# A Mamba-2 mixer with its state stepped every 64 tokens in place of every 128

## What is computed

```
proj = x @ in_proj_w.T            # gate, x|B|C, dt
hBC  = silu(causal_conv4(proj[x|B|C]))
dt   = clip(softplus(dt + dt_bias));  A_cum = cumsum(dt * A) in a chunk
Y_diag = (C_l . B_s) * exp(A_cum[l]-A_cum[s]) * (s<=l) @ (x*dt)
states = sum_s B_s * exp(A_cum[-1]-A_cum[s]) * (x*dt)_s
prev'  = prev * exp(A_cum[-1]) + states
Y_off  = exp(A_cum[l]) * (C_l @ prev)
y = (Y_diag + Y_off + D*x) * silu(gate);  y = group_rms_norm(y) @ out_proj_w.T
```

## Time and profile before

| | us |
|---|---|
| median of 3 runs | 1868.56 (1868.19 to 1874.12) |
| time of the profiled execution | 1870.32 |
| its span, first to last instruction | 1868.5 |
| mean granted TensorE clock | 0.988 |

### The profile page before, as it was taken

How to read it: one execution, slowest core, us unless ns; L and a number is a source line. 1 busy time by engine, 2 the same in 40 slices (tenths; PEclk the granted TensorE clock), 3 DMA queues, 4 the chain that set the end, 5 groups by cost and what they waited for, 6 DMA issues and landing times.

```text
span 1868.5 us, 31134 instructions
## 1 busy us (share of the span) xinstructions
PE 1754.7 (94%) x9656; PEld 1344.0 (72%) x9656; DVE 1290.5 (69%) x2095; ACT 1065.5 (57%) x1946; POOL 942.1 (50%) x721
## 2 busy tenths in 40 slices
PE   6799999999999999999999999999999999999966
PEld 5567777777777777777777777777777777777755
DVE  5766667666766677766676667666777666766788
ACT  6566555656646565665546566465656555565632
POOL 2355453556535464554535555355644545455563
PEclk9899999999999999999999999999999999999988
DMA  6412121111202121121211212121211212111121
GB/s 224 130 30 69 55 66 44 50 60 57 66 28 72 49 66 51 35 66 55 66 45 48 62 54 68 29 72 45 70 51 29 72 55 66 44 48 61 34 96 57
DMA packets 77097, 114.14 MB, mean 61 GB/s; under 512 B 21376, under 2 KB 28032, under 8 KB 76032
## 3 DMA queue, kind: packets, MB, share of 16 engines
q1 hardware_dynamic: 59360, 80.06, 14.2%
q10 hardware_dynamic: 17568, 31.99, 5.1%
HBM read 88.94 MB, written 23.07 MB: 60 GB/s over the span
## 4 chain that ended last, share of the span: by engine, by line
issue 46%; POOL 34%; PE 9%; DVE 5%; ACT 3%; DMA 1%; SPq 1%; POOLq 1%; ACTq 0%; DVEq 0%
POOL yt L1605 9%; POOL ssq L1600 7%; POOL wg_lo L1524 4%; POOL wo_lo L1524 4%; POOL prev L1586 3%; POOL yt L1608 3%; POOL wx_lo L1524 3%; PE bank L476 2%; PE bank L478 2%; PE bank L477 2%; PE bank L641 1%; PE bank L706 1%; DMA raw_w<-w_in_dram 1%; PE bank L840 1%; ACT lm L1072 0%
## 5 line engine op out<-in xcount | busy, mean ns | idle before, releaser
L1605 POOL TENSOR_TENSOR yt<-yt,ea 128x384 f32<-128x384 f32 (+1 forms) x128 | 189.6, 1481 | 393.1 <-DVE ea L1440 393.1
L1218 DVE SCALAR_TENSOR_TENSOR xc<-bank,bpar,xc 128x511 f32<-128x511 f32 (+2 forms) x384 | 285.4, 743 | 52.8 <-ACT xc L906 48.3
L1410 DVE TENSOR_TENSOR lm<-lm,cbm 128x512 f32<-128x512 f32 x256 | 185.9, 767 | 155.7 <-ACT lm L1075 155.7
L476 PE MATMUL bank<-h_hi,wg_hi 128*128 128x512 f32 x640 | 262.0, 409 | 31.3 <-ACT gate L1030 21.9
L478 PE MATMUL bank<-h_hi,wg_lo 128*128 128x512 f32 x640 | 251.0, 392 | 0.0
L477 PE MATMUL bank<-h_lo,wg_hi 128*128 128x512 f32 x640 | 250.2, 391 | 0.0
L476 PE MATMUL bank<-wo_hi,g_hi 128*128 128x512 f32 x496 | 206.9, 417 | 7.2 <-POOL wo_lo L1524 7.2
L476 PE MATMUL bank<-h_hi,wx_hi 128*128 128x512 f32 x512 | 210.3, 411 | 2.2 <-DVE bt L1218 2.2
L1586 POOL TENSOR_TENSOR prev<-prev,dec 128x512 f32<-128x512 f32 x96 | 102.0, 1063 | 206.0 <-DVE prev L1356 131.9
L478 PE MATMUL bank<-h_hi,wx_lo 128*128 128x512 f32 x512 | 200.3, 391 | 0.0
L477 PE MATMUL bank<-h_lo,wx_hi 128*128 128x512 f32 x512 | 199.9, 390 | 0.0
(11 more groups left out here) (187 smaller groups left out, 3796.9 us busy)
## 6 DMA issues: line engine op xcount, KB each, us to landing
raw_w<-w_in_dram SPq DMA_DIRECT2D x145, 256.0 KB, 2.6
raw_w<-w_out_dram SPq DMA_DIRECT2D x64, 256.0 KB, 2.6
part_d<-part ACTq DMA_DIRECT2D x64, 256.0 KB, 2.0
part<-part_d ACTq DMA_DIRECT2D x58, 256.0 KB, 2.7
rt<-rows_d SPq DMA_DIRECT2D x256, 8.0 KB
acc<-x_dram SPq DMA_DIRECT2D x8, 256.0 KB, 6.6
acc<-w_mod_dram SPq DMA_DIRECT2D x2, 1024.0 KB, 6.0
lh<-neg_d SPq DMA_DIRECT2D x128, 8.0 KB
```

The costliest lines, as they stand in the source:

```text
L476: nc.tensor.matmul(out_ap, whi(k), hhi(k), start=(k == 0), stop=False)
L1218: stt(dst[:, at], ps[:, 0:HALF - 3 + k], w(k), dst[:, at], ALU.mult, ALU.add)\
L1410: tt(lm[:, h % 4, :], lm[:, h % 4, :], cbm[:, toks(hf)], ALU.mult).then_inc(v_m, 1)
L1605: tt(yt[:, j % 2, cols], yt[:, j % 2, cols], ea[:, j % 2, cols], ALU.add).then_inc(p_t3, 1)
```

## The change

The chunk in which the state is stepped becomes 64 tokens (`SUB`); z still counts 128-token pieces, k counts 64-token pieces, s is the first or second half of a z.

- `diff`: one pair of products per j (two heads, 256 columns each, one row group) in place of two products of 512 columns. Both land in bank 2.
- Relu, Exp and `mix` are one per j in place of two, each still 128 x 512: two heads' 64 x 64 masks lie side by side.
- Masked products: for each z four products of 64 rows, 64 stationary and 64 moving columns, one in each quarter of the array, the token halves to two banks.
- Products with old states: for each 64 tokens one product with 128 stationary and 64 moving columns: 7 or 8 per j in place of 3 or 4.
- State products: for each z two products of 64 rows and 512 columns, in the array's row halves, to banks 6 and 7; now also for z = 3 of the second half (its first 64 tokens).
- DVE: `new_state` 8 or 7 per unit in place of 4 or 3; `xw` also for z = 3; yt in two pieces of 256. POOL: 7 decays per unit in place of 3. SP: 17 small loads per unit in place of 13.
- The C.B products are 16 of 64 x 64 in a group in place of 8 of 128 x 128.

The core of the diff:

```diff
+SUB = CHUNK // 2
+NS = HALF // SUB
...
-        prev = sb("prev", [128, NZ + 1, BLOCK])
-        lm = sb("lm", [128, 4, HALF])
+        prev = sb("prev", [128, NS, BLOCK])
+        lm = sb("lm", [128, 2, HALF])
```

SyncE, `unit_params`:

```diff
+                for j in range(NCT):
+
+                    e = 32 * EA_ROWS[j] + SROWS
+                    rsub = rsrc[j, 0:4, toks(hf)].rearrange("r (z s l) -> s r z l", z=NZ, s=2)
+                    for s in range(2):
+                        at = 32 * j + 4 * s
+                        sp.dma_start(rt[p][at:at + 4, 0:NZ * SUB].bitcast(F).rearrange("r (z l) -> r z l", z=NZ),
+                                     rsub[s]).then_inc(d_par[p], 16)
+                    sp.dma_start(rt[p][e:e + 4, :].bitcast(F), rsrc[j, 4:8, toks(hf)]).then_inc(d_par[p], 16)
```

TensorE, `states`, `diff`, the products with the old states and the masked products:

```diff
+                        te.wait_ge(v_prev, ab0 + 2 * z)
+                    for s in range(1 if hf == 1 and z == NZ - 1 else 2):
+                        lst = nc.tensor.matmul(bank[6 + s][:, :], bt[sub_rows(s), toks(hf, z, 1)],
+                                               xw[sub_rows(s), z % 2, :], start=True, stop=True)
+                    lst.then_inc(t_st, 1)
...
+                    for i in range(2):
+                        lst = nc.tensor.matmul(bank[2][:, i * NZ * SUB:(i + 1) * NZ * SUB],
+                                               lh[par_][32 * j:32 * j + SROWS, i * 128:(i + 1) * 128],
+                                               rt[par_][32 * j:32 * j + SROWS, 0:NZ * SUB], start=True, stop=True)
+                    lst.then_inc(t_diff, 1)
...
-                if hf == 0:
-                    states(3)
+                states(3)
...
-                        te.wait_ge(v_prev, sb0 + 3)
...
+                        te.wait_ge(v_prev, ab0 + NS - 1)
...
-                    for z in range(1 - hf, NZ):
-                        lst = nc.tensor.matmul(bank[6][:, chunk(z)], prev[:, slot(hf, z), j * 128:(j + 1) * 128],
-                                               ct[:, toks(hf, z, 1)], start=True, stop=True)
+                    for k in range(1 - hf, NS):
+                        lst = nc.tensor.matmul(bank[6][:, k * SUB:(k + 1) * SUB],
+                                               prev[:, slot(k), j * 128:(j + 1) * 128],
+                                               ct[:, subtoks(hf, k)], start=True, stop=True)
...
                     for z in range(NZ):
-                        for i in range(2):
-                            h = 2 * j + i
-                            lst = nc.tensor.matmul(bank[5][64 * i:64 * i + 64, chunk(z)],
-                                                   xdt[:, z, h * HDIM:(h + 1) * HDIM], lm[:, h % 4, chunk(z)],
-                                                   start=True, stop=True)
+                        for i, s in ((0, 0), (1, 1), (1, 0), (0, 1)):
+                            h, at = 2 * j + i, (i * NZ + z) * SUB
+                            lst = nc.tensor.matmul(yd[64 * i:64 * i + 64, s, z * SUB:(z + 1) * SUB],
+                                                   xdt[sub_rows(s), z, h * HDIM:(h + 1) * HDIM],
+                                                   lm[sub_rows(s), j % 2, at:at + SUB], start=True, stop=True)
```

VectorE, the order in a unit:

```diff
+                    if z == 3:
+                        new_state(3)
...
                     if z >= 1:
-                        new_state(z - 1)
+                        new_state(2 * z - 2)
...
+                    if z == 1:
+                        new_state(1)
...
                 mix(0)
-                mix(1)
+                new_state(5)
+                new_state(6)
                 if not first and not end:
                     accumulate(u, g1, b1, h1, 3)
                 if hf == 0:
-                    new_state(3)
+                    new_state(7)
```

GpSimd, the order in a unit:

```diff
+                if hf == 1:
+                    decay(0)
+                for f in todo[0] + todo[1]:
+                    unit_fill(f, g)
+                decay(1)
+                decay(2)
+                for f in todo[2]:
+                    unit_fill(f, g)
+                for k in range(3, NS - hf):
+                    decay(k)
+                for f in todo[3]:
+                    unit_fill(f, g)
```

More of the change, by code:

```diff
@@ L327, in _ @@
             xt = x.rearrange("(t p) n -> t p n", p=128)
-            mods = [flat(xdt, 0, 4), flat(gate, 0, 4), flat(prev, 0, 4), flat(lm, 0, 4), flat(acc, 0, 4), flat(acc, 4, 8)]
+            mods = [flat(xdt, 0, 4), flat(gate, 0, 4), flat(prev, 0, 4), flat(prev, 4, 8), flat(acc, 0, 4), flat(acc, 4, 8)]
             def load_mod(v):
@@ L501, in mod_row @@
                 te.wait_ge(d_mod[v], 16)
-                t, k0 = ((xdt, 0), (gate, 0), (prev, 0), (lm, 0), (acc, 0), (acc, 4))[v]
+                t, k0 = ((xdt, 0), (gate, 0), (prev, 0), (prev, 4), (acc, 0), (acc, 4))[v]
                 for k in range(NK):
@@ L630, in unit @@
                 par_, end = hf, last and c == 3
-                sb0 = states_before(nb, hf)
+                ab0 = adds_before(nb, hf)
                 def states(z):
[L634 to L638, removed]
-                    else:
-                        te.wait_ge(v_prev, sb0 + z)
-                    nc.tensor.matmul(bank[7][:, :], bt[:, toks(hf, z, 1)], xw[:, z % 2, :],
-                                     start=True, stop=True).then_inc(t_st, 1)
@@ L644, in diff @@
[L644 to L656 removed]
+                    te.wait_ge(v_xw, 4 * u + z + 1)
@@ L679, in group_bc @@
                     for h2 in range(2):
-                        for zz in range(NZ):
-                            lst = nc.tensor.matmul(bank[2 + h2][:, chunk(zz)], bt[:, toks(h2, zz, 1)],
-                                                   ct[:, toks(h2, zz, 1)], start=True, stop=True)
-                        lst.then_inc(t_cb, 1)
+                        for k in range(NS):
+                            at = (h2 * NZ + k // 2) * SUB
+                            lst = nc.tensor.matmul(bank[2][sub_rows(k % 2), at:at + SUB], bt[:, subtoks(h2, k)],
+                                                   ct[:, subtoks(h2, k)], start=True, stop=True)
+                    lst.then_inc(t_cb, 1)
                     if first:
@@ L970, in _ @@
             keep_row(3)
-            se.wait_ge(v_scan, 2)
-            for z in range(NT):
-                lst = act(ea[:, z // 4, chunk(z % 4)], xw[:, z // 4, chunk(z % 4)], ACT.Exp, scale=-1.0,
-                          bias=xw[:, z // 4, (z % 4 + 1) * 128 - 1:(z % 4 + 1) * 128])
-            lst.then_inc(a_fe, 1)
+            se.wait_ge(v_drop, 1)
+            act(flat(ea, 0, 2), flat(ea, 0, 2), ACT.Exp).then_inc(a_fe, 1)
             pro_split(5)
@@ L1434, in unit @@
                     ge(ve, v_lo, 4 * u + j - 1)
-                    stt(yt[:, j % 2, :], xc[:, j, :], par(c // 2, j, SKIP), bank[5][:, :], ALU.mult, ALU.add)\
-                        .then_inc(v_t2, 1)
+                    for s in range(2):
+                        lst = stt(sub_first(yt[:, j % 2, :])[:, s], sub_first(xc[:, j, :])[:, s], par(c // 2, j, SKIP),
+                                  yd[:, s, 0:NZ * SUB].rearrange("p (z l) -> p z l", z=NZ), ALU.mult, ALU.add)
+                    lst.then_inc(v_t2, 1)
                     ve.wait_ge(t_yo, 4 * u + j + 1)
@@ new lines, in unit @@
+                if not first and c in (0, 3):
+                    group_rstd(g - 1 if c == 0 else g, 1 if c == 0 else 0)
+                if hf == 1:
[10 more added lines that the diff above has]
+                    unit_fill(f, g)
```

217 lines of the change are left out of this document (111 added, 106 removed).

## The result

The changed kernel takes 2056.6 us (median of 4 runs, 2051.4 to 2057.5), the kernel before 1870.7 in the same series: a ratio of 1.0987, 95% interval 1.0958 to 1.1015. That is 186 us slower. The forecast was 1986, with a range to 2055: the direction was right, but the increase was 186 us and not 116, and the time lies just above the range.

A forecast was written before the change was run, and what follows sets the result against it. The prediction took TensorE, busy 94% of the span, to bound the kernel. 1870.3 + 106 of TensorE work + 32 of chain waits - 22 of relieved waits gave 1986 us, range 1945 to 2055.

The forecast's parts named there:

- Old-state products: On TensorE: 1024 more instructions at 0.11 us each, the price of taking up 128 stationary columns, +113 us.
- Rival 4: On TensorE: loads of stationary operands hide whole at any length and shape, 1836 us; chance 0.03.
- State products: On TensorE: row halves run side by side, shape changes cost 38 us and 16 more products 14, +52 us.
- Rival 5: State products on TensorE: the row halves run one after the other, +110, 2096 us; chance 0.03.
- Masked products: On TensorE: eight rounds of four quarters at half the pace save 0.44 us a group, -55 us.
- rivals 2 and 3: Masked products: quarters run only two at a time, 2041 us, chance 0.08; instruction issue bounds them, 2155 us, chance 0.04.
- C.B and row products: On TensorE: C.B products in 16 rounds plus an excursion, -4 us; row products of the differences as long as before, 0.
- Other engines: ScalarE -160 us, VectorE near 1300 to 1340, GpSimd near 1080; none becomes the bound, SP's extra loads are covered.
- The chain at the end of the z phase: TensorE waits 0.4 us for new_state(5) and 0.4 for new_state(6); taken as 1.0 per unit, +32 us.
- The chain within the z phase: Between state products: two links of 3.9 us are covered by 4.4 us of TensorE work, with 0.5 to spare.
- Rival 1: State chain decides: two GpSimd weight splits per unit fall into it, 58 us more, 2044 us; chance 0.17.
- What comes back: On TensorE: waits for VectorE's acc go, -11.0, and half of those on the gate, -11, together -22 us.

The follow-up runs named there:

- before_late_wait: The kernel before, with the first old-state products in first-half units waiting for the unit's last new state: 1892.8 us, ratio 1.0111.
- narrow_alone: The kernel before, with each old-state product cut into two of 64 moving columns, nothing else: 1925.5 us, ratio 1.0292.
- cut_projection: The changed kernel, with the j phase's first projection split ahead of the last state product and the first old-state products: 1987.4 us, ratio 1.0621.
- wide_again: The changed kernel, with old-state products of 128 moving columns again, every second 64 tokens' states left out of them: 1961.0 us, ratio 1.0470.

## Why the prediction was right and wrong

- **Old-state products**, forecast +113: the trace has 28.9 - 15.6 = 13.3 a group, +106. Right. By rows it came from a product with one moving column. The Trainium skill, TensorE: Matmul & The Clock Gate, section LDWEIGHTS (loading the stationary operand), makes it a matter of stationary columns, and the trace agrees with 0.12 us an instruction at 64 moving columns. Rival 4, which let these loads hide, is refuted.
- **State products**, forecast +52: 3.4 a group and 1.2 in the steps into them, +37. The run prices the shape alone: 30, forecast 38. The mechanism was right, the size too high: I gave an excursion 0.4, but a pair takes 0.20 more than a whole product and the step into it 0.10 more, 0.3 together. The Trainium skill, TensorEngine Tiling (Array Packing), section Tiling Modes (Key Properties), says that a change of tiling mode drains the engine; the step of 0.32 in place of 0.22 into a pair agrees. Rival 5 is refuted.
- **Masked products**, forecast -55: -6.3 a group, -50; the run says 47. Right; rivals 2 and 3 are refuted.
- **C.B and row products**, -4 and 0: -0.7 a group and 0.0. Right.
- **Other engines**: none became the bound; SP's four loads cost nothing that the waits show. Right, but ScalarE fell by 110 us, not 160: I took the mean durations of a Relu and an Exp, 0.60 and 0.65, which overlap; by their busy time, 138.8 and 149.2 for 256 each, half of them is 144 at most.
- **The chain at the end of the z phase**: forecast 0.4 and 0.4 us. On the trace TensorE waits 0.4 before the last state product (0.69 from start to start, 764.54 to 765.23, where 0.32 is usual) and 0.44 before the old-state products. Right; the sum took 1.0 a unit, 32 us, where these are about 0.8, 26 us.
- **The chain within the z phase** is the first failed step: "A state product waits for two links, 3.9 us ... so 4.4: covered by 0.5 in the z phase." That took GpSimd as free. In c = 3 the new order puts a third split ahead of `decay(1)`. Rival 1 had named the splits, but at 0.9 us for each of two in every unit, and set against it that "decays 1 and 2 stand ahead of the third split", which is a wrong reading: in c = 3 there are six splits, and the two lists ahead of `decay(1)` hold three. It was one wait of 4.4 us in seven groups, over the 2 us that the prediction named as a sign of being wrong, because the split stands on weights that are late in both kernels. Moving that one loop body was worth 46 us.
- **The clock** is the second and larger failed step. The text says once that the loop ran at full granted clock, and the sum then prices every step at it. No term, bound or rival let the clock fall. It cost 61 us, a third of the increase. The Trainium skill, TensorE: Matmul & The Clock Gate, section A second HAM failure mode, tells of a kernel whose clock swings because TensorE stands idle briefly between groups of products. The trace of the changed kernel agrees, with waits of 0.44 and 0.35 us ahead of a stretch at 0.51; `before_late_wait` doesn't, with no fall behind the 12 waits that it adds in the loop.
- **What comes back**: forecast -22. The waits for `acc` and the gate went as said, and `narrow_alone` shows what was there to give: 30 us of waits in all, for 84 of work.

Without the clock the sum of what was measured is 1870 + 78 + 51 = 1999, within the range.

What stays open: whether a wait lowers the clock or the unbroken run of sparse products around it, because `cut_projection` took out both; and what the row halves add, because 64-column products with waits and whole state products were not tried. `wide_again` shows that row halves and quarters with the same short waits, but without the narrow products, kept full clock. Why the clock fell with c = 1 and not with c = 2 isn't known either.

## What to carry to other kernels

A product that is cut along its moving side keeps its stationary load: here, with 128 stationary columns, an instruction cost 0.11 to 0.12 us with 1, 64 and 128 moving ones. So ask for each product which side a shorter chunk shortens. When a serial chain gets twice the links, go through every engine on it for what stands ahead of each link in program order, and for the latest arrival that this item may itself wait for. And when the engine that bounds gets new waits of half a microsecond between sparse products, give the stretch behind them at half clock a price of its own, at least as a bound: here it came behind about half of them.

## What the runs showed of the hardware that was not expected

- Waits of 0.3 and 0.44 us around row-half and 64-column products were followed by stretches at 0.5 of the clock in 13 of 24 units; with those behind the long wait they made 17.6 us a group at half clock in the changed kernel. With 128-column products in place of the 64-column ones the same waits were followed by none in c = 0 to 2; with the short waits covered by half a projection each, and the long one cut to 1.2, the narrow products ran at full clock throughout the loop.
- Four 64 x 64 quarters, each with its own stationary operand, ran 32 instructions in 0.62 us, 0.02 each.
- Adding 896 instructions, 84 us of work by the trace, to the engine that was 94% busy lengthened the kernel by 54 us.
